# A grouped 3x3 convolution on 96 partitions and four 32-column pieces, with norms on POOL and ACT and later weight loads

## The reference, cut to what matters

```
x = x + relu(conv3x3(layernorm(x), groups=8) + bias)        # stage A, the one that is changed
t = t + experts_B(layernorm(t))     # 32 experts, each takes its best 128 of 4096 tokens
x = x + window_attention(layernorm(x))                      # 16 heads, windows of 8 x 8
t = t + experts_D(layernorm(t))     # 8 experts, top 2 per token
```

## Time and profile before

| what | us |
|---|---|
| median of 3 runs | 795.96 (795.4 to 797.33) |
| the profiled execution | 797.43 |
| its span in the profile | 795.6 |
| first gate instruction (end of stage A) | 102.28 |
| first POOL gather (end of the rank search) | 214.79 |
| mean granted TensorE clock | 0.79 of full |

### The profile page before, as it was taken

One profiled execution on the slowest core, in us unless ns is written; L12 is line 12 of the kernel. 1 busy time (PEld: TensorE's weight loads), 2 busy tenths in 40 slices (PEclk: granted clock), 3 DMA queues, 4 the chain that ended last, 5 costly groups with the idle time before them and its releaser, 6 DMA issues.

```text
span 795.6 us, 12900 instructions
## 1 busy us (share of the span) xinstructions
PE 520.7 (65%) x4447; PEld 413.3 (52%) x4447; DVE 473.6 (60%) x1178; ACT 264.1 (33%) x627; POOL 372.4 (47%) x345
## 2 busy tenths in 40 slices
PE   4999722223484665069999978415978887878850
PEld 2455521111153544037777758314867877878840
DVE  5365568898711112298999997695535344444427
ACT  1122133322522121037777774121323223223225
POOL 2000000000168887347888862065676666676740
PEclk9999855555877787558999996555999889898995
DMA  9700145000035453720000002450111111111129
GB/s 302 304 26 28 50 84 149 0 0 0 9 97 138 97 142 34 171 54 2 2 4 2 3 2 80 94 144 23 38 44 41 44 43 42 40 46 39 47 65 285
DMA packets 65245, 56.04 MB, mean 70 GB/s; under 512 B 10176, under 2 KB 59200, under 8 KB 65056
## 3 DMA queue, kind: packets, MB, share of 16 engines
q1 hardware_dynamic: 49904, 38.45, 16.9%
q0 software_dynamic: 10688, 14.04, 8.4%
q10 hardware_dynamic: 4592, 2.75, 1.3%
HBM read 35.37 MB, written 19.86 MB: 69 GB/s over the span
## 4 chain that ended last, share of the span: by engine, by line
PE 31%; POOL 20%; DVE 18%; issue 17%; DMA 6%; another core or an unknown queue 4%; ACT 3%; DVEq 0%; SPq 0%; POOLq 0%; ACTq 0%
PE psum L1351 7%; POOL arena L556 6%; PE psum L1608 6%; PE psum L1625 5%; PE psum L1330 4%; PE psum L1614 4%; DVE arena_b L738 3%; POOL scratch L502 3%; POOL v_x L546 2%; DMA arena<-normed,gather_i 2%; POOL results L591 2%; POOL y_odd L512 2%; POOL x_tok L539 2%; POOL y_even L512 1%
## 5 line engine op out<-in xcount | busy, mean ns | idle before, releaser
L502 POOL DMA_INDIRECT scratch<-table,idx x32 | 33.8, 1055 | 218.2 <-DVE idx_w L852 208.7
L591 POOL DMA_INDIRECT results<-arena,dest_i x71 | 74.5, 1049 | 51.3 <-ACT arena L1307 33.6
L1108 DVE TENSOR_TENSOR arena<-arena,psum 128x384 f32<-128x384 f32 x71 | 39.2, 553 | 88.9 <-remote 31.7
L583 POOL DMA_INDIRECT arena<-normed,gather_i x71 | 78.2, 1101 | 26.9 <-issue 20.7
L1330 PE MATMUL psum<-cst,arena 128*128 128x128 f32 x327 | 58.1, 293 | 43.8 <-issue 17.7
L1301 ACT ACTIVATE arena<-psum 128x384 f32<-128x384 f32 x71 | 35.2, 495 | 124.0 <-PE psum L1608 85.0
L556 POOL TENSOR_TENSOR arena<-arena,peak 128x1024 f32<-128x1024 f32 x32 | 60.9, 1904 | 30.4 <-DVE peak L940 30.4
L1625 PE MATMUL psum<-arena_b,arena 128*128 128x128 f32 x426 | 67.9, 301 | 0.3 <-issue 0.2
L1330 PEld LDWEIGHTS psum<-cst,arena 128*128 128x128 f32 x327 | 41.8, 150 | 49.3 <-issue 41.2
L1608 PE MATMUL psum<-arena 128*128 128x128 f32 x426 | 66.2, 297 | 0.0
L1614 PE MATMUL psum<-arena 128*128 128x128 f32 x426 | 65.5, 292 | 0.5 <-issue 0.3
(11 more groups left out here) (236 smaller groups left out, 1116.7 us busy)
## 6 DMA issues: line engine op xcount, KB each, us to landing
arena<-in_w_down_dram SPq DMA_DIRECT2D x8, 768.0 KB
w_sb<-in_w_dram SPq DMA_DIRECT2D x3, 1536.0 KB, 13.9
x_tok<-in_x_dram SPq DMA_DIRECT2D x4, 512.0 KB, 7.8
y_odd<-zeros SPq DMA_DIRECT2D x4, 512.0 KB
table<-xn SPq DMA_DIRECT2D x8, 256.0 KB, 2.3
y_even<-x_tok SPq DMA_DIRECT2D x16, 128.0 KB
extra<-y_odd ACTq DMA_DIRECT2D x4, 512.0 KB, 11.5
x_tok<-y_even SPq DMA_DIRECT2D x4, 512.0 KB, 10.5
```

The costliest lines, as they stand in the source:

```text
L502: nc.gpsimd.indirect_dma_start(out=rows_b[:, e // 4 % 4, e % 4, :], out_offset=None, in_=table[:, :], in_offset=bass.IndirectOffsetOnAxis( ...
L583: nc.gpsimd.indirect_dma_start(out=rows_d[:, t % ROWS_D, :], out_offset=None, in_=normed[:, :], in_offset=bass.IndirectOffsetOnAxis(ap=gat ...
L591: nc.gpsimd.indirect_dma_start(out=results[:, :], out_offset=bass.IndirectOffsetOnAxis(ap=dest_i[:, t:t + 1], axis=0), in_=y_d[:, t % 4, : ...
L1108: nc.vector.tensor_tensor(act_d[:, b, :], silu_d[:, b, :], psum[:, 3 + b, 0:FF_D], ALU.mult).then_inc(e_act, 1)
```

## The change

The convolution uses that output channels 32q to 32q+31 need only input channels 32q to 32q+31. Per block:

- SP writes the padded images of the block from `scratch` to a DRAM buffer `padded`, waits for it, and reads it back three times, shifted by dx = 0, 1, 2, into partitions 32*dx to 32*dx+31 of one of three buffers `shifted` (two in `arena`, one in `arena_b`). In it the four quarters q of the channels lie one behind the other along the free dimension.
- For each of three rows dy and four quarters q, a matmul with 96 rows (32 channels x 3 shifts) and 32 output columns writes PSUM partitions 32q to 32q+31. These are 12 matmuls and not 9, and the weights shrink from 128 x 1152 to 96 x 384.

The norm of stage A moves from VectorE to POOL, that of stage B to ScalarE (as scale and bias of an activation). The lags of all pipelines grow, and the last iteration of TensorE is 14 and not 13. Ten of the weight loads are issued behind the last expert's weights, with waits for them in the attention stage, and the zeros of `y_odd` behind the copies to `y_even`. The last stage's results come back in 4 pieces and not 8. The scaling of the query bias moves from ScalarE to VectorE.

```diff
-TAPS = 9
+TAP_ROWS, TAP_COLS = 3, 3
+QUARTER = P // 4
+TAP_PARTS = TAP_COLS * QUARTER
+IMAGE = PAD * PAD
+SHIFTED = 2 * IMAGE - (TAP_COLS - 1)
...
+        shifted = [shared(pool_of, at, [P, 4, 2 * IMAGE])[0] for pool_of, at in
+                   ((arena, 0), (arena, 8 * IMAGE), (arena_b, 0))]
...
+        CONV_LOADS = [(ident, const[:, 0:P]), (conv_sb[0:TAP_PARTS], conv_w.rearrange("p (t q c) -> p t q c", t=TAP_ROWS, q=4)),
+                      (conv_bs[:], conv_b)]
+        LOADS = [(wr_sb[:], w_router), (br_sb[:], router_bias.partition_broadcast(P)), (bu_sb[:], up_bias),
+                 (cst[:, P:], const[:, P:])]
+        LATE_LOADS = [(wqkv[:], qkv_w), (qkb[:], qk_bias), (vb_sb[:], v_bias.partition_broadcast(P)),
+                      (rel[:, 0, :], rel_bias), (rel[:, 1, :], rel_bias), (msk[:], mask.rearrange("h p j -> p h j")),
+                      (gw[:], gate_w), (w13_sb[:, :, 0, :], w1), (w13_sb[:, :, 1, :], w3), (w2_sb[:], w2)]
...
-            sp.wait_ge(s_zero, 1)
-            for c in range(4):
-                sp.dma_start(y_odd.rearrange("(p line) c -> p (line c)", p=P)[:, 1024 * c:1024 * (c + 1)],
-                             zeros[:]).then_inc(b_init, 16)
+
+            def spread_block(n):
+
+                cols = slice(2 * IMAGE * n, 2 * IMAGE * (n + 1))
+                sp.wait_ge(a_pad, n + 1)
+                sp.dma_start(padded[:, cols], scratch[:, cols]).then_inc(a_out, 16)
+                sp.wait_ge(a_out, 16 * (n + 1))
+                if n > 2:
+                    sp.wait_ge(a_conv, n - 2)
+                by_quarter = padded.rearrange("(q p) f -> p q f", q=4)
+                for dx in range(TAP_COLS):
+                    at = 2 * IMAGE * n + dx
+                    sp.dma_start(shifted[n % 3][QUARTER * dx:QUARTER * (dx + 1), :, 0:SHIFTED],
+                                 by_quarter[:, :, at:at + SHIFTED]).then_inc(a_in[n % 3], 16)
 
             tab_v = table.rearrange("(t p) c -> p t c", p=P)
-            for n in range(BLOCKS):
+
+            def table_block(n):
                 sp.wait_ge(b_xn, n + 1)
                 sp.dma_start(tab_v[:, 4 * n:4 * n + 4, 0:P], xn[:, 1]).then_inc(b_tab, 16)
+
+            short_pipeline(BLOCKS, [(table_block, 5), (spread_block, 0)])
...
+            sp.wait_ge(s_pad, 2)
+            for c in range(4):
+                sp.dma_start(y_odd.rearrange("(p line) c -> p (line c)", p=P)[:, 1024 * c:1024 * (c + 1)],
+                             zeros[:]).then_inc(b_init, 16)
...
+            for dst, src in LATE_LOADS:
+                sp.dma_start(dst, src).then_inc(ld_late, 16)
...
-            for n in range(BLOCKS):
+            for c in range(4):
                 for k, dst in enumerate((back1, back2)):
-                    sp.dma_start(dst[:, 4 * n:4 * n + 4, :],
-                                 results_v[k, :, 4 * n:4 * n + 4, :]).then_inc(f_back[n], 16)
+                    sp.dma_start(dst[:, 8 * c:8 * c + 8, :],
+                                 results_v[k, :, 8 * c:8 * c + 8, :]).then_inc(f_back[c], 16)
...
+            for n in range(BLOCKS):
+                pool.wait_ge(a_rs, n + 1)
+                if n > 0:
+                    pool.wait_ge(a_tr, n)
+                for t in range(4 * n, 4 * n + 4):
+                    ins = nc.gpsimd.tensor_scalar(xn[:, 0, t % 4, :], x_tok[:, t, :], mean[:, t:t + 1], rstd[:, t:t + 1],
+                                                  ALU.subtract, ALU.mult)
+                ins.then_inc(a_xn, 1)
...
-            def norm_a(n):
-                if n > 0:
-                    dve.wait_ge(a_tr, n)
-                block_norm(n, 0, a_sqrt, a_xn)
+            def scale_a(n):
+                dve.wait_ge(a_sqrt, n + 1)
+                tiles = slice(4 * n, 4 * n + 4)
+                nc.vector.reciprocal(rstd[:, tiles], std[:, tiles]).then_inc(a_rs, 1)
...
-            short_pipeline(BLOCKS, [(variance_a, 0), (norm_a, 0), (norm_b, 4), (residual, 3), (variance_b, 3)])
+            def scale_b(n):
+                tiles = slice(4 * n, 4 * n + 4)
+                inverse_root(tiles, b_sqrt, n + 1)
+                nc.vector.scalar_tensor_tensor(recentre[:, tiles], mean[:, tiles], -1.0, rstd[:, tiles], ALU.mult,
+                                               ALU.mult).then_inc(b_rs, 1)
+
+            short_pipeline(BLOCKS, [(variance_a, 0), (residual, 4), (variance_b, 4), (scale_a, 0), (scale_b, 4)])
...
-            short_pipeline(BLOCKS, [(lambda n: block_root(n, a_var, a_sqrt), 0), (pad, 0), (relu, 2),
-                                    (lambda n: block_root(n, b_var, b_sqrt), 4), (evac_b, 5)])
+            def norm_b(n):
+                act.wait_ge(b_rs, n + 1)
+                if n > 0:
+                    act.wait_ge(b_tr, n)
+                    act.wait_ge(b_tab, 16 * n)
+                for t in range(4 * n, 4 * n + 4):
+                    ins = nc.scalar.activation(xn[:, 1, t % 4, :], x_tok[:, t, :], ACT.Identity, bias=recentre[:, t:t + 1],
+                                               scale=rstd[:, t:t + 1])
+                ins.then_inc(b_xn, 1)
+
+            short_pipeline(BLOCKS, [(pad, 1), (norm_b, 5), (lambda n: block_root(n, a_var, a_sqrt), 0),
+                                    (evac_b, 6), (relu, 3), (lambda n: block_root(n, b_var, b_sqrt), 4)])
...
-                if n == 0:
-                    pe.wait_ge(ld_conv, 16 * len(CONV_LOADS))
-                pe.wait_ge(a_pad, n + 1)
+                pe.wait_ge(a_in[n % 3], 16 * TAP_COLS * (n // 3 + 1))
                 if n > 1:
                     pe.wait_ge(a_relu, n - 1)
-                for tap in range(TAPS):
-                    dy, dx = tap // 3, tap % 3
-                    ins = nc.tensor.matmul(psum[:, 2 + n % 2, :], conv_sb[:, tap, :],
-                                           xpad[:, 2 * n:2 * n + 2, dy:dy + SIDE, dx:dx + SIDE],
-                                           start=tap == 0, stop=tap == TAPS - 1)
+                for dy in range(TAP_ROWS):
+                    for q in range(4):
+                        pixels = shifted[n % 3][0:TAP_PARTS, q, :].rearrange("p (i a b) -> p i a b", i=2, a=PAD)
+                        ins = nc.tensor.matmul(psum[QUARTER * q:QUARTER * (q + 1), 2 + n % 2, :],
+                                               conv_sb[0:TAP_PARTS, dy, q, :], pixels[:, :, dy:dy + SIDE, 0:SIDE],
+                                               start=dy == 0, stop=dy == TAP_ROWS - 1)
                 ins.then_inc(a_conv, 1)
...
-            short_pipeline(BLOCKS, [(transpose_a, 0), (transpose_b, 5), (convolve, 1), (transpose_back, 2),
-                                    (route, 6)])
+            short_pipeline(BLOCKS, [(convolve, 3), (transpose_b, 6), (transpose_back, 4), (transpose_a, 0), (route, 7)])
```

More of the change, by code:

```diff
@@ L362, in metaformer @@
         a_res = sem("a_res")
+        a_rs, b_rs = sem("a_rs"), sem("b_rs")
+        a_out = sem("a_out")
+        a_in = [sem(f"a_in{i}") for i in range(3)]
         b_xn, b_tr, b_xt, b_logit = (sem(f"b_{s}") for s in ("xn", "tr", "xt", "logit"))
@@ L396, in metaformer @@
         e_st = [sem(f"e_st{i}") for i in range(4)]
-        f_back = [sem(f"f_back{i}") for i in range(BLOCKS)]
+        f_back = [sem(f"f_back{i}") for i in range(4)]
         f_sum = sem("f_sum")
@@ L491, in _ @@
             nc.gpsimd.memset(scratch[:], 0.0).then_inc(s_pad, 1)
-            nc.gpsimd.memset(zeros[:], 0.0).then_inc(s_zero, 1)
+            nc.gpsimd.memset(zeros[:], 0.0).then_inc(s_pad, 1)
+            for n in range(BLOCKS):
[6 more added lines that the diff above has]
+                ins.then_inc(a_xn, 1)
             pool.wait_ge(b_tab, 16 * BLOCKS)
@@ L647, in block_variance @@
                 variance(tiles, var_ready, eps)
-            def block_norm(n, slot, sqrt_done, ready):
-                inverse_root(slice(4 * n, 4 * n + 4), sqrt_done, n + 1)
-                for k in range(4):
-                    ins = norm(xn[:, slot, k, :], 4 * n + k)
-                ins.then_inc(ready, 1)
             def variance_a(n):
@@ L879, in heads @@
                 return ap.rearrange("p (h j) -> p h j", j=WIN)
+            dve.wait_ge(ld_late, 16 * len(LATE_LOADS))
             for w in range(2):
@@ L1543, in _ @@
             pe.wait_ge(c_one, 2)
+            pe.wait_ge(ld_late, 16 * len(LATE_LOADS))
             def gate_block(n):
@@ L1649, in lay_out @@
     width = k.shape[2]
-    conv = np.zeros((P, TAPS, P), k.dtype)
-    for g in range(P // width):
-        s = slice(g * width, (g + 1) * width)
-        conv[s, :, s] = k.reshape(TAPS, width, P)[:, :, s].transpose(1, 0, 2)
+    conv = np.zeros((TAP_COLS, QUARTER, TAP_ROWS, 4, QUARTER), k.dtype)
+    for co in range(P):
+        q, o = divmod(co, QUARTER)
+        i = o // width * width
+        conv[:, i:i + width, :, q, o] = k[:, :, :, co].transpose(1, 2, 0)
     up = a["L0_ffn_W_up"]
```

37 lines of the change are left out of this document (13 added, 24 removed).

## The result

The changed kernel takes 812.88 us (811.55 to 814.48, 4 runs) against 796.64 (795.4 to 798.43, 4 runs) beside it: ratio 1.0192, 95% interval 1.0163 to 1.0221. The profiled execution took 811.55 us with a span of 809.7. Forecast were 779.3 us, range 763 to 797.

What follows compares the result with a forecast made beforehand. Prediction: TensorE's convolutions bound the first stage, then the DMA loop would. Gate minus 21.6 us plus 5 for held scatter-adds gave minus 16.6: 780.8 us profiled from 797.43, 779.3 as a median; range 763 to 797.

Steps and rivals of the forecast that it cites:

- Convolution: TensorE, first stage: 24 records with four pieces side by side take 2.7 us a block instead of 7.73.
- Rival 3: TensorE's column pieces run one after the other, 12.4 us a block, gate plus 28; 829 us, chance 0.09.
- near 22: Sign that the forecast is right: the convolution's records on TensorE are busy for near 22 us in all.
- The circle: First stage, round through engines and DRAM: three blocks in 14.7 us, 4.9 a block, below the 6.0 us DMA pace.
- DMA loop: First stage, SP's queue: write, wait and three reads set the pace, 6.0 us a block, 6.9 with a table write.
- POOL's norm: First stage, POOL: four tensor_scalars of 0.46 us, 1.8 a block, beside the DMA transfers except 0.7 us in block 0.
- 80.7: End of the first stage: the first gate instruction starts at 80.7 us instead of 102.3, minus 21.6.
- The clock: TensorE, first stage: at 1.2 GHz the round of three blocks takes 18.3 us, or 6.1 a block.
- Late loads: Ten loads behind the last expert's weights hold up POOL's scatter-adds: plus 5 us, ends 0 and plus 11.
- Results in four pieces, early weights, zeroing: Kernel end: 0, at most plus 2; loads off the first 36 us cost nothing there; y_odd zeros free before POOL's gather.
- Rival 2: Slow reads in the first stage and held scatter-adds: minus 14.4 us with 9 given back; 790.5 us, chance 0.14.

Runs made afterwards that it cites:

- e1: Changed kernel with VectorE's first-norm scale ahead of the residual and ScalarE's first-norm root first: 806.28 us, ratio 1.0077 to the kernel before.
- e3: Changed kernel with the ten late weight loads issued earlier, during the rank search: 809.42 us, ratio 1.0121 to the kernel before.
- e5: Changed kernel with both repairs, scale ahead of residual and ten loads during the rank search: 766.69 us, ratio 0.9913 to the kernel before.
- e11: Repaired kernel without DRAM hop, two table buffers, norm on VectorE, plus 8 useless TensorE products a block: 770.11 us, ratio 0.9937 to the kernel before.
- e12: Repaired kernel without DRAM hop, two table buffers, norm on POOL, plus 8 useless TensorE products a block: 772.17 us, ratio 0.9978 to the kernel before.
- after_same_chip: The changed kernel itself run again beside the experiments, nothing altered: 789.8 us, ratio 1.0197 to the kernel before.
- e4: Kernel before with only the ten weight loads moved behind the last expert's weights: 810.69 us, ratio 1.0145 to the kernel before.
- e15: Changed kernel, both repairs, no DRAM hop, norm on VectorE, block copies issued half by SyncE, half by POOL: 753.98 us, ratio 0.9728 to the kernel before.
- e18: The kernel of e15 with ScalarE's norm writing to two buffers in turn: 749.5 us, ratio 0.9668 to the kernel before.
- e14: Changed kernel with both repairs, padded-block DRAM write issued by ScalarE, two norm buffers, norm on POOL: 762.36 us, ratio 0.9829 to the kernel before.

## Why the prediction was wrong

**Convolution: right.** 2.71 us at 2.4 GHz for 24 records against 2.7 forecast. Rival 3, the serial pieces, is out. 10.3 / 2.71 is 3.8 pieces side by side. The convolution's records are busy for 36 us in all and not for the near 22 that the prediction named as a sign, as the first six blocks took 4.7 to 5.4 us each. The Trainium skill (TensorE: Matmul & The Clock Gate, the part on packing small matmuls) has 2.38 times for three column pieces; for four float32 ones the trace has more than that rule scaled.

**The circle: the step that failed.** The prediction said of POOL and VectorE that "All of this lies beside the DMA loop" and of the round through all engines that it holds three blocks, "14.7 us, 4.9 a block". The division by three was wrong: the round of the trace carries one block in 12.2 to 14.8 us. That its length is near 14.7 is luck. The prediction's round follows a block's data through DRAM to its own convolution three blocks on, with 7.8 us of DMA and no norm in it, and on TensorE at 1.2 GHz it was 18.3. The round of the trace has no DMA, 3.1 us of POOL's norm and most of its convolutions at 1.2 GHz: it goes from `transpose_a(k)` straight on to convolution k-2, which stands behind it in TensorE's list. VectorE issues residual(k-4) ahead of scale_a(k), TensorE's convolve(k-3) stands ahead of transpose_back(k-4) and behind transpose_a(k-1). So scale_a(k) waits for convolution k-3, and convolution k-2 waits for scale_a(k). Once the first four blocks have filled the lag, one block passes per round. The block starts show it: 22.6, 29.0, then 41.2, 54.6, 68.8, 83.6, and again 90.1, 94.6 when no new scale_a is left. e1 took this order away (with ScalarE's root moved to the head of its list to match), and the gate moved to 96.9, by 11.9 us from e3 or 16.0 from the first trace, of the 28.1 or 32.2 us by which these lie above 80.7. Of the 16.2 us that are left between 80.7 and 96.9, 10.3 lie between the first and the last convolution (55.0 us where the forecast had 44.7), in the DMA loop below.

**The DMA loop: mis-sized.** The reads were taken at 310 GB/s and 3.2 us; they ran at 204 GB/s for 4.8 us, above the upper end of 4.1. The loop is then 1.4 + 4.8 + 1.0 + 0.4 = 7.6 us where 6.0 stood; e5 has 7.36. In the changed kernel this lies under the circle and is not seen; it is the limit for the first five blocks of e1 and e5. The 6.9 that the prediction gave to a block with a table write was too little as well: ScalarE's norm waits for that write, and the sixth block of e5 comes 11.8 us after the fifth. Behind the row of 204 GB/s stands the rule that the prediction set aside: the Trainium skill (SBUF — State Buffer, Door 1: The DMA port swizzle) gives 218 GB/s for 32 neighbouring partitions, and here the trace agrees. I scaled up a rate of 87 GB/s from 16 copies that follow each other in one queue; that they overlap, and for that reason show more than the rule gives, is a guess that no run tests. By the prediction's own estimate the rule would have put the stage's gain at 10 us, near half of mine.

**POOL's norm: mis-sized.** 0.46 us taken, bounds 0.34 and 0.61, measured 0.79: 3.13 us a block instead of 1.8. In the circle, where the prediction had no norm at all, all 3.13 us count in every round. The row for POOL that it was taken from was an addition of two tensors, another operation.

**The clock.** The prediction had the circle at 18.3 us with TensorE at 1.2 GHz. It ran at that level (0.50 from 40 to 70 us, convolutions of 5.2 us). e11 and e12 show that lifting the clock with useless work gave no gain where SyncE's queue is on the chain. In the changed kernel's circle the convolution is on the chain, and there the clock counts: at 0.67 instead of 0.54 between 40 and 80 us (after_same_chip and e3) the third to the sixth convolution took 2.0 and 2.3 us less together, and the gate came 3.2 and 4.1 us earlier. An estimate from these rows says that it is not the whole loss: with convolutions of 2.71 instead of 5.21 us and the round's 2.15 us of transposes unchanged or halved, the round of 13.2 us would be 10.7 or 9.7, still above the 9.22 of the kernel before. No run had the changed order at a full clock.

**Late loads: mis-sized by a factor of two.** Plus 5 forecast, plus 10.4 in the trace, 9.8 alone in e4, inside the stated ends 0 and 11. The landing under company was sized from one small read (1.1 us longer); it was 6 us longer per add. The mechanism, adds held by loads of another queue, was right.

**Results in four pieces, early weights, zeroing:** no loss in the stretches where they lie, as forecast; none was tested alone. From the start of the last scatter of stage four to the end the two kernels need 25.6 and 25.7 us.

**Adding up.** Gate +10.6, adds +10.4, the other stretches -6.9, in all +14.1; the forecast had -21.6 and +5. In the other kernels the shift of the gate and the change of the stretch of the adds, both against the kernel before, give the difference of the medians within 3.3 us: e1 -5.4 + 10.3 = +4.9, measured +5.4; e15 -19.6 - 0.9 = -20.5, measured -20.5; e18 -23.6 - 0.9 = -24.5, measured -24.6; the largest misses are e14 (-8.8, measured -12.1) and e11 (-1.9, measured -4.8). Only the first profile of the changed kernel has 21.0 where 16.2 were measured; with the gate of after_same_chip it is 17.5 against 15.7. In the first profile the gate is late, with the low clock described above, and the stretch of stage four's gathers, which the change does not touch, gives 4.0 us back. TensorE's granted clock between 700 and 770 us was 0.98 there against 0.93; what made that difference stays open.

**The rivals.** Rival 2 had both sizes nearly right, slow reads and adds held for 9 us. It too came out faster than before, at 790.5, since it took the pace from the DMA loop and divided its circle by three. No case of the forecast had the order of the engines as its mechanism.

## What to carry to other kernels

Before a pace is taken from the slowest stage, write down for each in-order engine what stands behind which wait for one step of the pipeline, and count how many blocks can be in the round: a lag of three in the order is worth nothing when the first entry of a step waits for the last. A work item that feeds the head of the pipeline goes ahead of one that waits for its tail; here that order was worth 12 to 16 us at the gate. A DMA has three separate prices: its bytes at the rate of the partitions they reach, its place in the queue, and the 0.4 to 0.6 us of the engine that issues it. A single buffer can put an idle engine on the chain: here ScalarE's norm waited for a table write that stood behind the reads. Big loads are put where no chain of small dependent transfers runs beside them.

## What was not expected of the hardware

- POOL needs 793 ns for a tensor_scalar with two per-partition operands over 128 float32 columns, against 343 ns on VectorE (32 and 64 instructions).
- Scatter-adds of POOL's queue land 9.4 to 9.6 us after their issue while SyncE's queue moves 353 to 378 GB/s, and 3.6 us without.
- A DMA between 32 partitions of SBUF costs SyncE 0.63 us from issue to issue; POOL issues six of the same in 2.93 us, 0.49 each (e15).
- The changed kernel took 812.88 us at first and 789.8 us later, and 21.6 of the 22.0 us between the two traced spans are in stage four (208.3 and 186.7 us from its first gather to its last). The kernel before moved as much beside it. What makes the two levels is open; the record has one chip number at both.
